# Three orders changed in an attention and routing tower: three TensorE matmuls, two ScalarE casts, one GpSimd chain

## The chip, the cores and the metric

One core of one Trainium2 chip. The metric is the device time of one execution in microseconds (us). Five engines work side by side and meet through semaphores: TensorE (PE; its weight loads have rows of their own, PEld), VectorE (DVE), ScalarE (ACT), GpSimd (POOL) and SyncE (SP, which only issues DMAs here).

## The reference, cut to what matters

`x` holds 128 samples of 375 x 512 floats. Each sample is cut into q, k and v of 125 rows each.

```python
weight = softmax(einsum('bct,bcs->bts', q * scale, k * scale))   # 512 x 512 for each sample
h = einsum('bts,bcs->bct', weight, v)                            # 125 x 512
h = h + attn(layernorm(h), Wq, Wk, Wv, Wo)                       # rotary, soft-capped tanh, 8 heads, 2 kv heads
y = layernorm(h)
out = h + (silu(y @ sw1) * (y @ sw3)) @ sw2                      # shared expert, width 448
        + top-2-of-8 experts of y                                # routed experts w1, w2, w3
```

All matmuls that matter keep 32-bit accuracy by splitting each operand into a high part (rounded to the fast 32-bit format of TensorE) and a low part (the rest), and multiplying high x high, high x low and low x high.

## The kernel before, in words

The kernel has two stages. The first, the tower, does one sample a step. The second runs the routed experts in groups of 512 rows. The change touches the tower alone.

A step `t` works on four samples at once, each at another point of its way: `has(0)` is sample t (512 x 512 scores, softmax, blend with v), `has(1)` is sample t-1, called a (first layernorm, qkv projection, rotary, attention), `has(2)` is sample t-2, called f (output projection, second layernorm, shared expert, routing), `has(3)` is sample t-3, called g (last part of the shared expert, output). There are 131 steps in all, 126 of which (t = 2 to 127) hold both a sample of `has(0)` and one of `has(2)`.

Each engine has its instructions for a step in an order written out by hand; nothing is planned at run time. An engine executes them in that order and stops at each `wait_ge` until the named semaphore has the value. So an instruction that is put earlier in the order of its engine can start earlier, and everything that it is moved past starts behind it.

The names that the change and its surroundings touch:

- TensorE: `scores(i)` (L433, three matmuls of 128 x 512) is one of four blocks of scores. `scores(2)` and `scores(3)` write into the PSUM bank from which ScalarE has to have read block 0 or 1 first (`e_sb`). `down_part(k, 1)` (L418) are matmuls of sample g's shared expert that write to bank 6. The transposes of X (L478), of `xn` and `y` (L408), the output projection `woT` (L345, 12 matmuls), the q part of `wqkv` (L345, 12 of width 512), the kv part (12 of width 256), and `turn_weights` (L444), which turns the normalised softmax weights `e`.
- ScalarE: `weights(i)` (L619) is the exponential of block i with its row sum; `vT_high` (L643) is the high part of the values, `xT_hi` (L599) the high part of the normed rows, which the q product waits for.
- VectorE: `h2` (L763, the profile prints it as `h<-ps,h`), its statistics `st` and `ag` (L770), `y` (L778, second layernorm), `rz` (L783) and the four `e<-e,rz` (L786), which scale the softmax weights and for which `turn_weights(0)` waits.
- GpSimd: `rstd(b, ...)` is two one-column operations, `ve` (variance plus epsilon, L904) and `rs` (its power -0.5, L907). It is called once for sample a (first layernorm) and once for sample f (second layernorm, for which `y` waits). `vT_low` (L931) is the low part of the values, 128 x 500, first read by TensorE in the blend near the end of the step. Then follow two indirect DMAs (L941) that write routing entries, `qkr` (L949) and `qk_low` (L916).

SyncE loads the next sample and stores two results of 250 KB in each step; none of its code is touched.

Of the kernel before, what the change touches and what calls it, by code (L numbers as in the profile page):

```python
# [25 lines left out]
ACT = mybir.ActivationFunctionType  # L26
# [45 lines left out]
def audio_tower(nc, x, wq, wk, wv, wo, gate_w, w1, w2, w3, sw1, sw2, sw3, expert_bias, cos, sin, out):  # L72
# [28 lines left out]
    with ExitStack() as ctx:  # L101
# [40 lines left out]
        vT = [sbuf(f"vT_{part}", [P, KC, C], F32R, tower) for part in ("high", "low")]  # L142
# [113 lines left out]
        def one(name, shape, dt=F32):  # L256
            return sbuf(name, shape, dt, tower)
# [9 lines left out]
        vT_full = one("vT_full", [P, KC, C])  # L267
# [3 lines left out]
        st2, ag2 = one("st2", [P, 6]), one("ag2", [P, 2])  # L271
        ve1, rs1 = one("ve1", [P, 1]), one("rs1", [P, 1])
        ve2, rs2 = one("ve2", [P, 1]), one("rs2", [P, 1])
# [36 lines left out]
        s_ps, o_ps, pv_ps = signal("s_ps", 2), signal("o_ps"), signal("pv_ps", 2)  # L310
        rank_ps, dn_ps, aT_ps = signal("rank_ps"), signal("dn_ps"), signal("aT_ps")

        xT_hi, vT_hi, yT_hi, v_sb, th_sb = (signal(n) for n in ("xT_hi", "vT_hi", "yT_hi", "v_sb", "th_sb"))
        ex_sb, e_sb, qkT_hi, hT_hi = signal("ex_sb"), signal("e_sb", KC), signal("qkT_hi"), signal("hT_hi")
        tanh_sb, p_sb = signal("tanh_sb", 2), signal("p_sb", 2)
        aT_hi, qk_hi, e_hi, vT_sb = signal("aT_hi"), signal("qk_hi"), signal("e_hi", KC), signal("vT_sb")

        h_sb, st1_sb, ag1_sb, xn_sb = signal("h_sb"), signal("st1_sb"), signal("ag1_sb"), signal("xn_sb")
        h2_sb, st2_sb, ag2_sb, y_sb = signal("h2_sb"), signal("st2_sb"), signal("ag2_sb"), signal("y_sb")
# [8 lines left out]
        ve1_sb, rs1_sb, ve2_sb, rs2_sb = signal("ve1_sb"), signal("rs1_sb"), signal("ve2_sb"), signal("rs2_sb")  # L328
# [37 lines left out]
        with nc.Block() as block:  # L366
# [37 lines left out]
            def _(pe):  # L404
# [7 lines left out]
                def step(t, has, n):  # L412
                    a, f, g = back(t, 1), back(t, 2), back(t, 3)
                    p = t[1] % 2

                    def down_part(k, part, c=0, last=False):

                        return nc.tensor.matmul(ps[0:C, 6, :], hT[c][0:HW, k, 0:C], w2s[part][0:HW, k, 0:D],  # L418
                                                start=(k == 0 and part == 0 and c == 0), stop=last)

                    def scores(i):

                        if i == 0:
                            pe.wait_ge(qk_hi.sem, qk_hi.at(t))
                            pe.wait_ge(qk_lo.sem, qk_lo.at(t))
                            pe.wait_ge(e_lo.sem, e_lo.at(a))
                        elif i == 1:
                            pe.wait_ge(h_sb.sem, h_sb.at(a))
                        else:
                            pe.wait_ge(e_sb.sem, e_sb.at(t, i - 1))  # L430
                        qk = (qk_high[p], qk_low)
                        for n_, (b, c) in enumerate(PASSES):
                            last = nc.tensor.matmul(ps[:, (i + 1) % 2, :], qk[b][0:C, 0, i * P:(i + 1) * P],  # L433
                                                    qk[c][0:C, 1, :], start=(n_ == 0), stop=(n_ == 2))
                        last.then_inc(qk_ps.sem, 1)
# [37 lines left out]
                    if has(0):  # L473
# [4 lines left out]
                            last = nc.tensor.transpose(ps[:, 2, k * C:(k + 1) * C],  # L478
                                                       X[p][0:C, 2, k * P:(k + 1) * P], ident[0:C, 0:C])
                        last.then_inc(vT_ps.sem, 1)  # L480
                    if has(0):
                        scores(2)
                    if has(3):
                        for k in range(1, HC):
                            down_part(k, 1)
                    if has(0):
                        scores(3)
                    if has(2):
# [108 lines left out]
            def _(act):  # L597
                def hi_part(dst, bank, rows):
                    return nc.scalar.activation(dst[0][0:rows, :, 0:C],  # L599
                                                ps[0:rows, bank, 0:KC * C].rearrange("p (k c) -> p k c", k=KC), ACT.Copy)  # L600
# [8 lines left out]
                def step(t, has, n):  # L609
                    a, f = back(t, 1), back(t, 2)  # L610
# [23 lines left out]
                    if has(0):  # L634
                        act.wait_ge(vT_ps.sem, vT_ps.at(t))
                        act.wait_ge(vT_lo.sem, vT_lo.at(a))
                        nc.scalar.activation(vT_full[:, :, :], ps[:, 2, 0:KC * C].rearrange("p (k c) -> p k c", k=KC),
                                             ACT.Copy).then_inc(vT_sb.sem, 1)
                        weights(2)
                        weights(3)  # L640
                        act.wait_ge(vT_sb.sem, vT_sb.at(t))
                        act.wait_ge(o_ps.sem, o_ps.at(a))
                        nc.scalar.activation(vT[0][:, :, :], vT_full[:, :, :], ACT.Copy).then_inc(vT_hi.sem, 1)  # L643
                    if has(1):
                        act.wait_ge(xT_ps.sem, xT_ps.at(a))
                        act.wait_ge(kv_ps.sem, kv_ps.at(f))
                        hi_part(xT, 3, P).then_inc(xT_hi.sem, 1)
                    if has(2):
                        act.wait_ge(yT_ps.sem, yT_ps.at(f))
                        act.wait_ge(up_ps.sem, up_ps.at(back(f, 1)))  # L650
                        hi_part(yT, 3, P).then_inc(yT_hi.sem, 1)
# [243 lines left out]
            @block.gpsimd  # L895
            def _(pool):
                last_entry = pool.to_reg(REGIONS - 1)

                def rstd(b, aggr, ve, rs, aggr_sb, ve_done, rs_done, rs_used):

                    pool.wait_ge(aggr_sb.sem, aggr_sb.at(b))
                    pool.wait_ge(rs_used.sem, rs_used.at(back(b, 1)))
                    alone(pool)
                    nc.gpsimd.tensor_scalar(ve[0:C, :], aggr[0:C, 1:2], EPS, None, ALU.add).then_inc(ve_done.sem, 1)  # L904
                    pool.wait_ge(ve_done.sem, ve_done.at(b))
                    alone(pool)
                    nc.gpsimd.tensor_tensor(out=rs[0:C, :], in0=ve[0:C, :], in1=mhalf[0:C, :],  # L907
                                            op=ALU.pow).then_inc(rs_done.sem, 1)

                def cut_scores(b):  # L910

                    q = b[1] % 2
                    pool.wait_ge(qk_hi.sem, qk_hi.at(b))
                    pool.wait_ge(qk_ps.sem, qk_ps.at(back(b, 1)))
                    alone(pool)
                    nc.gpsimd.tensor_tensor(out=qk_low[0:C, :, :], in0=X[q][0:C, 0:2, :],  # L916
                                            in1=qk_high[q][0:C, :, :].bitcast(F32),
                                            op=ALU.subtract).then_inc(qk_lo.sem, 1)

                def step(t, has, n):  # L920
                    a, f, g = back(t, 1), back(t, 2), back(t, 3)
                    if n == 0:
                        cut_scores(t)
                    if has(1):
                        rstd(a, ag1, ve1, rs1, ag1_sb, ve1_sb, rs1_sb, xn_sb)
                    if has(0):

                        pool.wait_ge(vT_hi.sem, vT_hi.at(t))
                        pool.wait_ge(o_ps.sem, o_ps.at(a))
                        alone(pool)  # L930
                        nc.gpsimd.tensor_tensor(out=vT[1][:, :, 0:C], in0=vT_full[:, :, :],  # L931
                                                in1=vT[0][:, :, 0:C].bitcast(F32),
                                                op=ALU.subtract).then_inc(vT_lo.sem, 1)
                    if has(2):
                        rstd(f, ag2, ve2, rs2, ag2_sb, ve2_sb, rs2_sb, y_sb)
                    if has(3):
                        pool.wait_ge(pick.sem, pick.at(g))
                        pool.wait_ge(place.sem, place.at(g))
                        alone(pool)
                        for k in range(2):  # L940
                            nc.gpsimd.indirect_dma_start(  # L941
                                routed, bass.IndirectOffsetOnAxis(ap=slot[g[1] % 2][0:C, k:k + 1], axis=0),
                                entry[k][g[1] % 2][0:C, :], None, bounds_check=last_entry,
                                oob_is_err=False).then_inc(scattered.of(g), 16)
                    if has(1):
                        pool.wait_ge(rope_sb.sem, rope_sb.at(a))
                        pool.wait_ge(rT_ps.sem, rT_ps.at(f))
                        alone(pool)
                        nc.gpsimd.tensor_tensor(out=qkr[0:C, :], in0=rc[0:C, :], in1=rsn[0:C, :],  # L949
                                                op=ALU.add).then_inc(rope_add.sem, 1)  # L950
                    if has(-1):
                        cut_scores(back(t, -1))
                each_step(pool, step)
                for b in ((0, NB - 2), (0, NB - 1)):
                    pool.wait_ge(scattered.of(b), scattered.at(b))
# [431 lines left out]
```

## Time and profile before

| | us |
|---|---|
| median of 3 runs | 6224.8 (6224.19 to 6226.47) |
| the profiled execution's own time | 6225.23 |
| its span in the trace | 6223.5 |
| TensorE busy | 6034.7 (97%) |
| VectorE busy | 3931.3 (63%) |
| ScalarE busy | 2617.3 (42%) |
| GpSimd busy | 2608.1 (42%) |

Busy time is the union of an engine's instructions. TensorE's matmuls are pipelined and their ends are modelled, so a wait of TensorE shows more fully before a weight load (PEld) than before a matmul. Times in the rows are counted from the span's start. The granted TensorE clock of the execution was 0.991 of full speed.

### The profile page before, as it was taken

What the parts mean: (1) busy time and instruction counts of PE and PEld (TensorE: products, weight loads), DVE (VectorE), ACT (ScalarE), POOL (GpSimd) and SP (SyncE); (2) the same over time, 40 slices, a digit from 0 to 9 for tenths busy, and PEclk for the clock granted to TensorE, in tenths of its full rate; (3) what the DMA queues carried; (4) which work ended last, traced back from release to release, by engine and by line L of the source; (5) the groups of instructions that cost most, each with busy time, mean ns of one, the idle gap of its engine ahead of it and who ended that gap; (6) DMA issues with size and microseconds to landing.
All of it is one profiled execution on the core that took longest, in us unless ns stands there. A gap on an engine that the chain in (4) does not pass through costs nothing. (4 is left out here: it accounts for less than half of the span.)

```text
span 6223.5 us, 108360 instructions
## 1 busy us (share of the span) xinstructions
PE 6034.7 (97%) x32968; PEld 5134.6 (83%) x32968; DVE 3931.3 (63%) x9812; ACT 2617.3 (42%) x4904; POOL 2608.1 (42%) x1865
## 2 busy tenths in 40 slices
PE   5999999999999999999999996999999999999999
PEld 4888888888888888888888885888888888888888
DVE  4777777777777777777777774444444444444444
ACT  3444444444444444444444442333333333333332
POOL 1333333333333333333333333555555655555554
PEclk8999999999999999999999998999999999999999
DMA  2111111111111111111111113555555555555541
GB/s 69 48 44 44 47 41 47 44 44 47 42 49 41 46 45 43 48 41 48 43 44 47 42 40 102 138 143 141 143 144 143 132 140 145 137 143 144 143 105 48
DMA packets 273407, 495.61 MB, mean 80 GB/s; under 512 B 39444, under 2 KB 112148, under 8 KB 273236
## 3 DMA queue, kind: packets, MB, share of 16 engines
q1 hardware_dynamic: 202452, 363.37, 19.6%
q0 software_dynamic: 70912, 131.71, 10.4%
q8 instruction: 22, 0.36, 0.0%
q14 instruction: 21, 0.17, 0.0%
HBM read 370.13 MB, written 140.28 MB: 82 GB/s over the span
## 5 line engine op out<-in xcount | busy, mean ns | idle before, releaser
L1325 POOL DMA_INDIRECT out_dram<-res,goal x280 | 519.4, 1855 | 929.9 <-DVE res L1261 446.1
L619 ACT ACTIVATE e<-ps,shift 128x512 f32<-128x512 f32 x512 | 347.9, 684 | 671.1 <-DVE shift L718 635.3
L1193 ACT ACTIVATE rT_hi<-ps 128x512 fp32r<-128x512 f32 x280 | 167.9, 600 | 1040.2 <-PE ps L1129 1040.2
L1119 PE MATMUL ps<-e_hi,rT_hi 128*128 128x448 f32 x2240 | 596.9, 388 | 5.2 <-ACT rT_hi L1193 5.2
L1303 POOL TENSOR_TENSOR e_lo<-raw,e_hi 128x1792 fp32r<-128x1792 f32 x140 | 568.6, 4062 | 9.8 <-ACT e_hi L1188 6.5
L1261 DVE COPY res<-ps 128x512 f32<-128x512 f32 x280 | 193.7, 692 | 594.8 <-PE ps L1119 579.8
L1119 PE MATMUL ps<-e_lo,rT_hi 128*128 128x448 f32 x2240 | 550.8, 367 | 0.0
L1119 PE MATMUL ps<-e_hi,rT_lo 128*128 128x448 f32 x2240 | 549.4, 367 | 0.0
L904 POOL TENSOR_SCALAR ve<-ag 125x1 f32<-125x1 f32 x256 | 57.1, 223 | 1124.7 <-DVE ag L734 1087.0
L1119 PEld LDWEIGHTS ps<-e_hi,rT_lo 128*128 128x128 f32 x2240 | 421.2, 188 | 37.8
L1119 PEld LDWEIGHTS ps<-e_lo,rT_hi 128*128 128x128 f32 x2240 | 421.2, 188 | 37.3
L931 POOL TENSOR_TENSOR vT_low<-vT_full,vT_high 128x500 fp32r<-128x500 f32 x128 | 164.8, 1287 | 588.4 <-ACT vT_high L643 588.4
L1275 DVE SCALAR_TENSOR_TENSOR ega<-eth,ps 128x448 f32<-128x448 f32 x280 | 174.0, 622 | 375.2 <-ACT eth L1214 369.1
L949 POOL TENSOR_TENSOR qkr<-rc,rsn 125x640 f32<-125x640 f32 x128 | 201.2, 1572 | 483.4 <-DVE rsn L814 483.4
L1119 PEld LDWEIGHTS ps<-e_hi,rT_hi 128*128 128x128 f32 x2240 | 380.5, 190 | 25.6 <-issue 5.6
L1214 ACT ACTIVATE eth<-ps,half 128x448 f32<-128x448 f32 x280 | 178.0, 636 | 516.7 <-PE ps L1119 515.0
L941 POOL DMA_INDIRECT routed_entries<-entry,slot x256 | 345.6, 1350 | 113.7 <-issue 100.9
L916 POOL TENSOR_TENSOR qk_low<-X,qk_high 125x1024 fp32r<-125x1024 f32 x128 | 307.2, 2400 | 203.7 <-ACT qk_high L606 203.7
L1188 ACT ACTIVATE e_hi<-raw 128x1792 fp32r<-128x1792 f32 (+1 forms) x210 | 372.6, 1774 | 40.3 <-DMA raw<-in_L_ffn_w 40.3
L715 DVE TENSOR_REDUCE negmax<-ps 128x1 f32<-128x512 f32 x512 | 341.1, 687 | 35.5 <-PE ps L433 22.0
L1282 DVE SCALAR_TENSOR_TENSOR egb<-ega,half,ps 128x448 f32<-128x448 f32 x280 | 190.5, 680 | 272.3 <-PE ps L1119 256.2
L626 ACT ACTIVATE e_cut_hi<-ps 128x512 fp32r<-128x512 f32 x512 | 277.2, 594 | 178.8 <-PE ps L444 177.6
(203 smaller groups left out, 15377.0 us busy)
## 6 DMA issues: line engine op xcount, KB each, us to landing
raw<-in_L_ffn_w SPq DMA_DIRECT2D x210, 896.0 KB, 5.6
X<-in_x SPq DMA_DIRECT2D x128, 750.0 KB
normed_rows<-y SPq DMA_DIRECT2D x128, 250.0 KB
out_dram<-h SPq DMA_DIRECT2D x128, 250.0 KB
rows<-normed_rows,entries POOLq DMA_INDIRECT x280, 4.8
out_dram<-res,goal POOLq DMA_INDIRECT x280
routed_entries<-entry,slot POOLq DMA_INDIRECT x256
raw<-in_L_ffn_sw SPq DMA_DIRECT2D x3, 896.0 KB
```

What stands on the lines that cost most here:

```text
L619: nc.scalar.activation(e[:, i, :], ps[:, (i + 1) % 2, :], ACT.Exp, scale=QS, bias=shift[:, i:i + 1], accum_out=total[:, i:i + 1]).then_inc ...
L626: nc.scalar.activation(e_cut[0][:, j, :], ps[:, j % 2, :], ACT.Copy).then_inc(e_hi.sem, 1)
L715: nc.vector.tensor_reduce(negmax[:, i:i + 1], ps[:, (i + 1) % 2, :], AX.X, ALU.max, negate=True).then_inc(max_sb.sem, 1)
L916: nc.gpsimd.tensor_tensor(out=qk_low[0:C, :, :], in0=X[q][0:C, 0:2, :], in1=qk_high[q][0:C, :, :].bitcast(F32), op=ALU.subtract).then_inc( ...
L941: nc.gpsimd.indirect_dma_start(routed, bass.IndirectOffsetOnAxis(ap=slot[g[1] % 2][0:C, k:k + 1], axis=0), entry[k][g[1] % 2][0:C, :], Non ...
L949: nc.gpsimd.tensor_tensor(out=qkr[0:C, :], in0=rc[0:C, :], in1=rsn[0:C, :], op=ALU.add).then_inc(rope_add.sem, 1)
L1119: ins = nc.tensor.matmul(dst, lhs[a][:rows_, k, :], rhs[b][:rows_, k, 0:width], start=(k == 0 and i == 0), stop=(k == KC - 1 and i == 2))
L1188: nc.scalar.activation(W[group[1] % 2][n][0][:], raws[n][:], ACT.Copy).then_inc(w_hi[n].sem, 1)
L1261: nc.vector.tensor_copy(res[i % 2][:], ps[:, 7, :]).then_inc(res_sb.sem, 1)
L1282: nc.vector.scalar_tensor_tensor(gb[i % 2][:], ga[:], half2[group[1] % 2][:, i:i + 1], ps[:, b + 1, 0:HID], ALU.mult, ALU.mult).then_inc(g ...
L1303: nc.gpsimd.tensor_tensor(out=W[group[1] % 2][n][1][:], in0=raws[n][:], in1=W[group[1] % 2][n][0][:].bitcast(F32), op=ALU.subtract).then_i ...
L1325: nc.gpsimd.indirect_dma_start(out, bass.IndirectOffsetOnAxis(ap=goal[group[1] % 2][:, i:i + 1], axis=0), res[i % 2][:], None, bounds_chec ...
```

## The change

Three blocks are moved to another place in the order of their engine. No instruction is added or removed.

```diff
 TensorE
-                    if has(0):
-                        scores(2)
                     if has(3):
                         for k in range(1, HC):
                             down_part(k, 1)
+                    if has(0):
+                        scores(2)
                     if has(0):
                         scores(3)
 ScalarE
                         weights(2)
                         weights(3)
+                    if has(1):
+                        act.wait_ge(xT_ps.sem, xT_ps.at(a))
+                        act.wait_ge(kv_ps.sem, kv_ps.at(f))
+                        hi_part(xT, 3, P).then_inc(xT_hi.sem, 1)
+                    if has(0):
                         act.wait_ge(vT_sb.sem, vT_sb.at(t))
                         act.wait_ge(o_ps.sem, o_ps.at(a))
                         nc.scalar.activation(vT[0][:, :, :], vT_full[:, :, :], ACT.Copy).then_inc(vT_hi.sem, 1)
-                    if has(1):
-                        act.wait_ge(xT_ps.sem, xT_ps.at(a))
-                        act.wait_ge(kv_ps.sem, kv_ps.at(f))
-                        hi_part(xT, 3, P).then_inc(xT_hi.sem, 1)
 GpSimd
                     if has(1):
                         rstd(a, ag1, ve1, rs1, ag1_sb, ve1_sb, rs1_sb, xn_sb)
+                    if has(2):
+                        rstd(f, ag2, ve2, rs2, ag2_sb, ve2_sb, rs2_sb, y_sb)
                     if has(0):
                         pool.wait_ge(vT_hi.sem, vT_hi.at(t))
                         pool.wait_ge(o_ps.sem, o_ps.at(a))
                         ...                       # vT_low, L931
-                    if has(2):
-                        rstd(f, ag2, ve2, rs2, ag2_sb, ve2_sb, rs2_sb, y_sb)
```

## Rows read from the trace of the kernel before

**Rows 1.** The page, busy time and share of the span of each engine.
```profile
PE 6034.7 (97%) x32968; PEld 5134.6 (83%) x32968; DVE 3931.3 (63%) x9812; ACT 2617.3 (42%) x4904; POOL 2608.1 (42%) x1865
```

**Rows 2.** One line's instructions, L643: durations in ns (min/median/max), first and last start.
```profile
L643 ACT ACTIVATE vT_high<-vT_full x128: 613/618/619, 68.7 to 3714.1; 128x500 fp32r<-128x500 f32 x128
```

**Rows 3.** Waits from 200 to 3700 us: us in total, times, longest.
```profile
PEld ps L433 <- ACT e L619: 86.9, 122, 0.8
...
PEld ps L345 <- issue: 31.9, 120, 0.3
```

**Rows 4.** Timeline of one step, weight loads: start, us, instruction [idle before <-releaser].
```profile
2011.64 0.58 PEld L478 LDWEIGHTS ps<-ident,X 125*128 125x128 f32 x4
...
2012.94 0.19 PEld L433 LDWEIGHTS ps<-qk_high 125*128 125x128 f32 x1 [0.72 <-ACT e L619]
...
2013.53 0.66 PEld L418 LDWEIGHTS ps<-w2s_lo,hT_hi 112*125 112x125 f32 x3
...
2014.22 0.19 PEld L433 LDWEIGHTS ps<-qk_high 125*128 125x128 f32 x1
...
2017.71 0.59 PEld L408 LDWEIGHTS ps<-ident,xn 125*128 125x128 f32 x4
...
2018.26 0.76 PEld L418 LDWEIGHTS ps<-w2s_hi,hT_lo 112*125 112x125 f32 x4
...
2019.29 0.75 PEld L345 LDWEIGHTS ps<-wqkv_hi,xT_hi 128*125 128x125 f32 x4 [0.27 <-issue]
...
2021.98 0.58 PEld L408 LDWEIGHTS ps<-ident,y 125*128 125x128 f32 x4
...
2024.15 0.86 PEld L444 LDWEIGHTS ps<-ident,e 128*128 128x128 f32 x8
```

**Rows 5.** Timeline of the same step, ScalarE.
```profile
2013.36 0.20 ACT L619 ACTIVATION_READ_ACCUMULATOR e<-ps,shift 128x1 f32 x1
...
2017.99 0.62 ACT L643 ACTIVATE vT_high<-vT_full 128x500 fp32r<-128x500 f32 x1
...
2018.57 0.59 ACT L599 ACTIVATE xT_hi<-ps 128x500 fp32r<-128x500 f32 x1
```

**Rows 6.** Timeline of the same step, VectorE and GpSimd.
```profile
2018.21 0.69 DVE L763 TENSOR_TENSOR h<-ps,h 125x512 f32<-125x512 f32 x1 [0.68 <-PE ps L345]
...
2018.81 1.29 POOL L931 TENSOR_TENSOR vT_low<-vT_full,vT_high 128x500 fp32r<-128x500 f32 x1 [4.51 <-ACT vT_high L643]
...
2019.82 0.18 DVE L770 BATCH_NORM_AGGREGATE ag<-st 125x2 f32<-125x6 f32 x1 [0.19 <-DVE st L766]
...
2020.27 0.22 POOL L904 TENSOR_SCALAR ve<-ag 125x1 f32<-125x1 f32 x1 [0.17 <-issue]
...
2020.68 0.57 POOL L907 TENSOR_TENSOR rs<-ve,mhalf 125x1 f32<-125x1 f32 x1 [0.18 <-POOL ve L904]
...
2021.38 0.55 DVE L778 TENSOR_SCALAR y<-h,ag,rs 125x512 f32<-125x512 f32 x1 [0.81 <-POOL rs L907]
2021.74 1.34 POOL L941 DMA_INDIRECT routed_entries<-entry,slot  x1 [0.50 <-issue]
...
2022.05 2.05 DVE L786 TENSOR_SCALAR e<-e,rz 128x512 f32<-128x512 f32 x4
```

**Rows 7.** Timeline of a window inside that group of four: its second instruction alone.
```profile
2022.45 0.86 DVE L786 TENSOR_SCALAR e<-e,rz 128x512 f32<-128x512 f32 x1
```

**Rows 8.** Timeline of step 0, where vT_low runs beside the scaling of e.
```profile
69.50 1.51 POOL L931 TENSOR_TENSOR vT_low<-vT_full,vT_high 128x500 fp32r<-128x500 f32 x1 [9.69 <-ACT vT_high L643]
69.83 1.46 DVE L786 TENSOR_SCALAR e<-e,rz 128x512 f32<-128x512 f32 x1
```

**Rows 9.** One line's instructions, L786, durations as in Rows 2.
```profile
L786 DVE TENSOR_SCALAR e<-e,rz x512: 467/482/1461, 69.0 to 3719.6; 128x512 f32<-128x512 f32 x171
```

**Rows 10.** Timeline of step 2, VectorE and GpSimd.
```profile
121.87 1.27 POOL L931 TENSOR_TENSOR vT_low<-vT_full,vT_high 128x500 fp32r<-128x500 f32 x1 [4.70 <-ACT vT_high L643]
123.11 0.22 POOL L904 TENSOR_SCALAR ve<-ag 125x1 f32<-125x1 f32 x1
...
124.79 1.68 DVE L786 TENSOR_SCALAR e<-e,rz 128x512 f32<-128x512 f32 x4
```

More of the change, by code:

```diff
@@ L640, in step @@
                         weights(3)
-                        act.wait_ge(vT_sb.sem, vT_sb.at(t))
-                        act.wait_ge(o_ps.sem, o_ps.at(a))
-                        nc.scalar.activation(vT[0][:, :, :], vT_full[:, :, :], ACT.Copy).then_inc(vT_hi.sem, 1)
                     if has(1):
@@ L647, in step @@
                         hi_part(xT, 3, P).then_inc(xT_hi.sem, 1)
+                    if has(0):
+                        act.wait_ge(vT_sb.sem, vT_sb.at(t))
+                        act.wait_ge(o_ps.sem, o_ps.at(a))
+                        nc.scalar.activation(vT[0][:, :, :], vT_full[:, :, :], ACT.Copy).then_inc(vT_hi.sem, 1)
                     if has(2):
```

## The prediction

> **What bounds the kernel now.** I read the page first. TensorE is busy for 97% of the span [rows 1], and the change only touches the tower, so the question is where TensorE stands still in one step of it. One instruction that each step holds once gives the period: the first start of `vT_high` is at 68.7 us, the last at 3714.1, with 127 steps between them, so 28.70 us a step [rows 2]. Next the waits: TensorE's weight loads wait for the exponential of block 0 in each of 122 steps, 86.9 us or 0.71 each, and in 120 steps 0.27 us ahead of a product of L345, put down to "issue" [rows 3]. Then the timeline of one step, which shows whether these waits are worth anything (times below are those of the step that begins near 2009; I leave the 2000 out). The first is ahead of `scores(2)`: the last transpose of X is loaded at 11.64 + 0.58 = 12.22, the scores start at 12.94. The second is ahead of the q product: the matmuls before it are loaded by 18.26 + 0.76 = 19.02, the product starts at 19.29 [rows 4]. `xT_hi` ends at 18.57 + 0.59 = 19.16 on ScalarE [rows 5], 0.13 before it. So I read the "issue" as the end of a wait for `xT_hi`: the pair of waits ahead of the product costs 0.13 after the cast. The reader is to see what follows: between the first stall and the second TensorE runs ahead of nothing. If the first stall goes alone, the second grows by the same amount.
>
> The third limit is not visible as a stall. `y` ends at 21.38 + 0.55 = 21.93 [rows 6], and TensorE loads it at 21.98, when its queue is also free (the product before takes 2.69). The scaling of `e` ends at 22.05 + 2.05 = 24.10 [rows 6], `turn_weights(0)` starts at 24.15 [rows 4]. Both are met to within 0.05 us. So in this step GpSimd's root, `y` and the four scalings form a chain that has no slack.
>
> **Part by part.**
>
> *Three matmuls ahead of `scores(2)`.* Their weight loads take 13.53 to 14.22, 0.69 [rows 4]; they fill the 0.72 of stall. `scores(2)` then starts at about 13.0 in place of 12.94, `scores(3)` at about 13.7 in place of 14.22 + 0.23; it needs exponential 1, which ends at 13.36 + 0.20 = 13.56 [rows 5]. Everything behind is up to 0.7 earlier, as far as the q product: the transposes of `xn` start at 17.0 in place of 17.71 and TensorE is free at 18.3 in place of 19.02. The output projection in between needs a cast that ScalarE starts behind exponential 1; with `xT_hi`'s 0.59 it is done by about 14.1, before the projection begins. By itself this part is worth 0, bounds 0 and 0.1 a step.
>
> *`xT_hi` ahead of `vT_high`.* ScalarE comes free at 17.99 and runs `vT_high` for 0.62 less overlap [rows 5]. With the order turned, `xT_hi` starts at 17.99, since the transposes of `xn` are now done by about 17.8, and ends at 18.58: 0.58 earlier. The q product starts at 18.71 in place of 19.29. With the first part this is -0.58 a step, bounds -0.4 (transposes late) and -0.7. `vT_high` ends at 19.2 in place of 18.61; behind it on ScalarE is only the cast of `y`.
>
> *The root of the second variance ahead of `vT_low`.* VectorE idles 0.68 ahead of `h2` [rows 6], so it can take nearly the whole advance: `h2` at 17.6, `ag` 0.6 earlier, `ve` at 19.67, `rs` from 20.08 to 20.65. Without this move `vT_low` would sit in front, so this keeps the chain early. What it costs is where `vT_low` lands. Before, it ran from 18.81 to 20.10, beside the statistics and `xT_lo` [rows 6]. Now its inputs are there long before and it starts when `rs` ends. GpSimd goes from one such operation to the next without a gap: `vT_low` from 121.87 for 1.27, the next at 123.11 [rows 10]. So `vT_low` holds 20.65 to 21.9. VectorE needs 0.13 from the end of `rs` to start `y` (20.68 + 0.57 = 21.25, `y` at 21.38), so `y` comes at 20.78, behind it.
>
> Step 0 shows what then happens. `vT_low` ran there beside the four scalings of `e`. The one that met it took 1.46 against a median of 0.48 [rows 8, 9], and ended at 71.29, 0.28 after `vT_low` did at 71.01. It was held for the whole rest of `vT_low`. The scalings are also held by the indirect DMAs of GpSimd: the second of four takes 0.86 [rows 7], and the group 2.05 against the 1.68 of a step without such DMAs [rows 6, 10]. `y` itself was never beside a GpSimd operation over the data. It belongs to the same form, I think: 512 elements from SBUF in 0.55, against 0.69 for `h2`, which reads PSUM [rows 6]. So `y` ends at 21.9 + 0.28 = 22.2 in place of 21.93. TensorE is ready for it at 21.4 and gets it at 22.2 + 0.13 = 22.32, in place of 21.98: +0.34. The 0.58 is given back, and a third of a us more.
>
> The Trainium skill, "SBUF — State Buffer", section "Who interferes with whom", says that VectorE in a two-port mode, which a `tensor_scalar` can enter, and a GpSimd operation shut each other out entirely, and that the one that issues first keeps the shared ports to its end. By that rule `y` waits as computed; if `y` were not of that form, the rule would leave it alone and only the scalings would meet `vT_low`. Rows 8 show the exclusion for `e`, none shows it for `y`.
>
> *Behind `y`.* The scalings start at about 22.3 and end at 22.3 + 2.05 = 24.35, since the DMAs now start at about 22.4 and still meet them; TensorE is ready for the transposes of `e` at 24.15 + 0.34 = 24.49. Hidden by 0.1; if the DMAs hold two scalings (0.38 each), it is 0.2 late. The DMAs' own shift of 0.7 is free: nothing on GpSimd follows until `qkr`, near 28.5, and `vT_low` is first read later than that. All that follows in the step hangs on TensorE and moves with it, so the +0.34 is the change of the period.
>
> **Sum.** 126 steps hold all parts: 126 x 0.34 = 43 us. On the profiled execution (6225.2, 0.4 above the median of the runs) that gives 6268; I take **6267**. The bounds of the terms give +0.2 to +0.5 a step: 6250 to 6288.
>
> **The rivals.**
>
> *No lockout, the gain stays.* If `y` and `vT_low` run side by side, or `vT_low` starts only after the scalings, the period falls by the 0.58 of the q product: 6225 - 126 x 0.58 = 6152. For it: `y` never showed a delay (nor had it occasion), and TensorE's stalls do lie where the three moves put them. Against: step 0. It decides at `y`: if it ends before 21.9, this comes in. 12%.
>
> *`y` first, the scalings held.* If GpSimd needs over 0.13 us to go from `rs` to `vT_low`, `y` runs from 20.78 to 21.33 and `vT_low` runs behind it to about 22.5. The first scaling ends at 22.8, the others at 23.9 to 24.4, where 24.10 was. TensorE was ready at 23.57. So -0.2 to +0.3 a step: 6200 to 6263, about 6232. For it: the DMA came 0.50 after `rs` [rows 6]. Against: the gapless pair of rows 10. 18%.
>
> *Worse.* `y` is held, and the scalings again, by the later DMAs: +0.55 a step, 6295. 5%.
>
> *The change doesn't do what it says.* If the transposes of `xn` are not done when ScalarE is free, or the advance of TensorE shrinks, the q product gains less than 0.58. That leaves `y` late just the same, since it hangs on `h2` and the root; the time stays in the forecast's range. 3%, to 6280.
>
> **How the numbers follow.** The forecast has 62%. The range of 6203 to 6288 leaves out the first rival and the worst one, and a part of the tails. Faster by over 0.2% (under 6212): the first rival's 12% and some of the second's low end, with a margin for what I overlooked in a chain this tight, 18%. Within 0.2%, about what can be told from no change: 12%, from the second rival. Slower: 70%.
>
> **What would show it.** In the profile after: the wait of L433 for `e` gone; `xT_hi` directly behind exponential 3, the q product 0.5 to 0.6 earlier from the step's start; a wait of 0.9 us ahead of the transposes of `y`; `y` at about 1.4 us in place of 0.55, in all steps from 2 on; `vT_low` directly behind `rs`; the four scalings still near 2.05. Wrong if `y` stays at 0.55: then the scalings tell which rival it is, at 2 us the first, at 3 us the second. Wrong in another way if TensorE's advance of 0.58 is not there at the q product.

## The result, and the profile after

The changed kernel takes 6253.6 us (median of 6 runs, 6247.4 to 6258.7), the kernel before 6225.7 beside it. The ratio is 1.0043, with a 95% interval of 1.0031 to 1.0055: slower by 28 us, 0.22 us in each of the 126 steps that hold all three parts. 6267 was forecast, in a range of 6203 to 6288. The profiled execution was the slowest of the six (6258.7, span 6256.9), so its trace shows 33 us and not 28.

First the same kind of row as [rows 2], of the changed kernel: the line of `vT_high` and, with it, those of `y` and of the scalings of `e`.

```profile
L648 ACT ACTIVATE vT_high<-vT_full x128: 614/624/624, 69.0 to 3748.5; 128x500 fp32r<-128x500 f32 x128
...
L779 DVE TENSOR_SCALAR y<-h,ag,rs x128: 546/1495/1505, 123.0 to 3800.6; 125x512 f32<-125x512 f32 x128
...
L787 DVE TENSOR_SCALAR e<-e,rz x512: 467/481/1461, 69.4 to 3753.7; 128x512 f32<-128x512 f32 x171
```

The steps take (3748.5 - 69.0) / 127 = 28.97 us against 28.70. That is the whole difference of the two spans. `y` takes 1.50 us in the median, where it took 0.55 [rows 6]; the scalings of `e` are as short as they were [rows 9]. `y` is long in all 126 steps that hold `vT_low` too, and has two lengths there: 1.40 to 1.42 in 60 of them and 1.50 in 66. It starts 0.14 after `rs` ends in the first and 0.03 in the second kind, and its end comes 0.28 to 0.29 after the end of `vT_low` in each of them.

The waits of TensorE's weight loads, 200 to 3700 us, columns as in [rows 3]:

```profile
PEld ps L408 <- DVE y L779: 97.9, 121, 0.9
...
PEld ps L345 <- issue: 45.2, 120, 0.4
...
PEld ps L444 <- DVE e L787: 42.7, 120, 0.4
...
PEld ps L433 <- ACT e L619: 26.5, 121, 0.3
```

The old stall ahead of the third block of scores has shrunk from 0.71 to 0.22 a step. Two new ones stand further down: 0.81 a step for `y`, 0.36 for the scalings. Now the timeline of one step of the changed kernel, which answers to the one in [rows 4 to 6]. Its scores begin at 2026.85; those of the step in [rows 4 to 6] began at 2009.48.

```profile
2026.85 0.19 PEld L433 LDWEIGHTS ps<-qk_high 125*128 125x128 f32 x1
...
2029.57 0.53 PEld L418 LDWEIGHTS ps<-w2s_lo,hT_hi 112*125 112x125 f32 x3
...
2030.31 0.19 PEld L433 LDWEIGHTS ps<-qk_high 125*128 125x128 f32 x1 [0.21 <-ACT e L619]
...
2034.93 0.69 DVE L764 TENSOR_TENSOR h<-ps,h 125x512 f32<-125x512 f32 x1
...
2035.35 0.59 ACT L599 ACTIVATE xT_hi<-ps 128x500 fp32r<-128x500 f32 x1
...
2036.07 0.75 PEld L345 LDWEIGHTS ps<-wqkv_hi,xT_hi 128*125 128x125 f32 x4 [0.37 <-issue]
...
2037.39 0.56 POOL L908 TENSOR_TENSOR rs<-ve,mhalf 125x1 f32<-125x1 f32 x1 [0.18 <-POOL ve L905]
...
2037.93 1.27 POOL L934 TENSOR_TENSOR vT_low<-vT_full,vT_high 128x500 fp32r<-128x500 f32 x1
...
2038.09 1.40 DVE L779 TENSOR_SCALAR y<-h,ag,rs 125x512 f32<-125x512 f32 x1 [0.80 <-POOL rs L908]
...
2039.55 0.41 PEld L408 LDWEIGHTS ps<-ident,y 125*128 125x128 f32 x4 [0.86 <-DVE y L779]
...
2039.61 2.10 DVE L787 TENSOR_SCALAR e<-e,rz 128x512 f32<-128x512 f32 x4
...
2040.88 0.55 PEld L345 LDWEIGHTS ps<-wqkv_hi,xT_lo 128*125 128x125 f32 x4
...
2041.77 0.31 PEld L444 LDWEIGHTS ps<-ident,e 128*128 128x128 f32 x3 [0.35 <-DVE e L787]
```

Counted from the first scores of its step, the changed kernel against the one before (us, one step of each):

| | before | after | |
|---|---|---|---|
| h2 starts | 8.73 | 8.08 | -0.65 |
| q product starts | 9.81 | 9.22 | -0.59 |
| rs starts | 11.20 | 10.54 | -0.66 |
| y starts | 11.90 | 11.24 | -0.66 |
| y ends | 12.45 | 12.64 | +0.19 |
| TensorE loads y | 12.50 | 12.70 | +0.20 |
| scalings end | 14.62 | 14.86 | +0.24 |
| TensorE loads e | 14.67 | 14.92 | +0.25 |

In both kernels `y` starts up to 0.2 earlier in other steps. The means of 110 steps say the same as the table: TensorE loads `e` at 14.59 before and at 14.87 after, +0.28.

So all three moves did what they were written for, down to the start of `y`. Then `y` took back 0.85. This is the lockout of the prediction: one engine's instruction cannot get on while the other engine's runs. `vT_low` starts at 2037.93, 0.02 before `rs` ends; `y` comes 0.14 after that end and is shown busy until 2039.49, 0.29 after `vT_low` ends at 2039.20. The reader should note how it looks: the held instruction has no idle time ahead of it, it is simply long. VectorE's busy time rose by 121 us (4052.4 against 3931.3) with the same instructions; 114 of them are `y`'s (184.2 against 70.0 in all), 6 the scalings'.

### The profile page after: what moved, and what is told of

It is laid out like the page before. It is cut to its first block and busy times, and to the rows that moved or that the text cites. A ratio compares the mean times of both kernels' runs of the same rounds, so it can differ in the third digit from the quotient of the medians.

```text
span 6256.9 us, 108360 instructions
## 1 busy us (share of the span) xinstructions
PE 6067.7 (97%) x32968; PEld 5105.1 (82%) x32968; DVE 4052.4 (65%) x9812; ACT 2605.7 (42%) x4904; POOL 2596.2 (41%) x1865
## 5 line engine op out<-in xcount | busy, mean ns | idle before, releaser
L725 DVE TENSOR_TENSOR e_cut_lo<-ps,e_cut_hi 128x512 fp32r<-128x512 f32 x512 | 329.2, 684 | 32.0 <-ACT e_cut_hi L626 32.0
```

The lines of the kernel that those rows point to most:

```text
L725: nc.vector.tensor_tensor(e_cut[1][:, j, :], ps[:, j % 2, :], e_cut[0][:, j, :].bitcast(F32), ALU.subtract).then_inc(e_lo.sem, 1)
```

## Experiments

Each was timed beside the kernel before. Its median was 6223.9 beside `vT_low` behind the DMAs, `vT_low` twice, TensorE's part alone and TensorE's and ScalarE's parts together, and 6226.2 beside the other four.

**The low part of the values behind the DMAs.** The changed kernel, GpSimd's order being root, DMAs, `vT_low`:

```diff
                     if has(2):
                         rstd(f, ...)
-                    ...                # vT_low
                     if has(3):
                         ...            # the two indirect DMAs
+                    if has(0):
+                        ...            # vT_low, with its waits
```

> The changed kernel with one thing moved: GpSimd's low part of the values goes behind the two indirect DMAs, so that it is no longer beside y and the scalings of e. Theory (y is locked out while vT_low runs): y falls back to 0.55 us, the 0.58 a step of the earlier q product is kept, about 6152 us, and at least 6170. Rival (the loss comes from the new order on TensorE or ScalarE, or from the root coming earlier): nothing changes against the changed kernel, about 6254.

Measured: 6146.1 us, ratio 0.9875 (0.9858 to 0.9891), within 6 us of the theory's number. In this kernel's timeline `y` and `vT_low` no longer meet:

```profile
2007.90 0.56 POOL L908 TENSOR_TENSOR rs<-ve,mhalf 125x1 f32<-125x1 f32 x1 [0.18 <-POOL ve L905]
...
2008.49 0.55 DVE L779 TENSOR_SCALAR y<-h,ag,rs 125x512 f32<-125x512 f32 x1 [0.65 <-POOL rs L908]
...
2011.94 1.28 POOL L943 TENSOR_TENSOR vT_low<-vT_full,vT_high 128x500 fp32r<-128x500 f32 x1
```

`vT_low` at 2011.94 runs beside VectorE instructions that read PSUM (`yT_lo`, 0.66 us there and 0.67 before); TensorE's waits for `y` and `e` are gone from the list, but for one wait for `y` in a single step. The kernel also holds its own counter-test. Step 2 has no DMAs yet, so `vT_low` stands directly behind `rs` in it, and there alone `y` is long:

```profile
124.64 0.56 POOL L908 TENSOR_TENSOR rs<-ve,mhalf 125x1 f32<-125x1 f32 x1 [0.18 <-POOL ve L905]
...
125.16 1.28 POOL L943 TENSOR_TENSOR vT_low<-vT_full,vT_high 128x500 fp32r<-128x500 f32 x1
125.23 1.50 DVE L779 TENSOR_SCALAR y<-h,ag,rs 125x512 f32<-125x512 f32 x1 [0.65 <-POOL rs L908]
```

The same three moves are worth -78 us with `vT_low` there, +28 with it one block earlier.

**vT_low twice.**

```diff
+        spare = one("spare", [P, KC, C])
...
                         alone(pool)
+                        nc.gpsimd.tensor_tensor(out=spare[:, :, 0:C], ...)    # same inputs
                         nc.gpsimd.tensor_tensor(out=vT[1][:, :, 0:C], ...)
```

> The changed kernel with vT_low computed a second time, into a spare tile, directly ahead of the real one: GpSimd works 1.27 us longer at this place, in a stretch where it otherwise idles 3.7 us later in the step. Theory: y is held for both, about 2.77 us in place of 1.50, and every step is 1.27 longer: 6254 + 126 x 1.27 = 6414 us. If the lock could be taken between the two, y is held by the first alone and the scalings by the second: 6350 to 6414. Rival (vT_low is hidden, its length does not matter): 6254.

Measured: 6342.4 us, 1.0191 (1.0174 to 1.0208), 89 us over the changed kernel in place of 160: 0.70 a step. It is the case named second, and it came out below the range given for it, 6350 to 6414. Timeline of this kernel:

```profile
2023.65 1.26 POOL L935 TENSOR_TENSOR spare<-vT_full,vT_high 128x500 f32<-128x500 f32 x1
...
2023.81 1.39 DVE L780 TENSOR_SCALAR y<-h,ag,rs 125x512 f32<-125x512 f32 x1 [0.80 <-POOL rs L909]
...
2024.87 1.45 POOL L938 TENSOR_TENSOR vT_low<-vT_full,vT_high 128x500 fp32r<-128x500 f32 x1
...
2025.32 2.72 DVE L788 TENSOR_SCALAR e<-e,rz 128x512 f32<-128x512 f32 x4
```

`y` slips in between the two, and now the second one is the longer, 1.45 in place of 1.27: it waited for `y`. Then it holds a scaling: the group takes 2.72 in place of 2.10. The 0.62 of that group is nearly all of the 0.70. Windows inside the group show its first and its fourth scaling alone, and the first DMA:

```profile
2025.32 1.29 DVE L788 TENSOR_SCALAR e<-e,rz 128x512 f32<-128x512 f32 x1
...
2026.53 1.28 POOL L946 DMA_INDIRECT routed_entries<-entry,slot  x1 [0.21 <-issue]
2027.32 0.72 DVE L788 TENSOR_SCALAR e<-e,rz 128x512 f32<-128x512 f32 x1
```

The first is held by `vT_low` for 0.81, the fourth by the DMA for 0.25, the other two take 0.47 each: 1.68 for the free group [rows 10] and 1.06 make 2.74. In the changed kernel only the second was held, by the DMA, for 0.44. So the second `vT_low` costs what it still covers of a scaling (0.81), and the later DMA holds a scaling for less. That is how 1.27 us more of GpSimd work became 0.62.

**y first.** The changed kernel with `vT_low` waiting for `y`:

```diff
                     if has(0):
+                        if has(2):
+                            pool.wait_ge(y_sb.sem, y_sb.at(f))
                         pool.wait_ge(vT_hi.sem, vT_hi.at(t))
```

> The changed kernel with one wait more: vT_low starts only when y is done, so that it meets the scalings of e in place of y. Theory (either is held, what counts is which of them TensorE needs first): y 0.55 us, one scaling about 1.5, the group of four about 2.8, TensorE waits ahead of the transposes of e and not of y; about 0.1 a step over the kernel before, 6237 us (6224 to 6270). If holding y was the whole loss and the scalings had slack: 6150.

Measured: 6219.9 us, 0.9991 (0.9982 to 1.0001), no change from before that these runs could tell, and 34 us under the changed kernel. The place is as expected, the time is 17 us under the 6237 and lies below the range given with it (6224 to 6270). Timeline:

```profile
2019.10 0.55 DVE L779 TENSOR_SCALAR y<-h,ag,rs 125x512 f32<-125x512 f32 x1 [0.81 <-POOL rs L908]
...
2019.77 2.70 DVE L787 TENSOR_SCALAR e<-e,rz 128x512 f32<-128x512 f32 x4
...
2019.93 1.47 POOL L936 TENSOR_TENSOR vT_low<-vT_full,vT_high 128x500 fp32r<-128x500 f32 x1 [0.96 <-DVE y L779]
...
2022.52 0.85 PEld L444 LDWEIGHTS ps<-ident,e 128*128 128x128 f32 x8 [0.74 <-DVE e L787]
```

`y` is short, the group of four pays with 2.70 (2.8 was expected), and TensorE waits ahead of `e` and not of `y`: 0.64 in the mean of 122 steps, 0.74 in the one shown. In the means of 110 steps it loads `e` at 14.56 after the scores, against 14.59 before, so nothing is won or lost. This was the second rival of the prediction, made to happen: its price there was 6232.

**The parts alone.** Each is the kernel before with one part (or two) of the diff above and nothing else.

TensorE's part alone:

```diff
-                    if has(0):
-                        scores(2)
                     if has(3):
                         for k in range(1, HC):
                             down_part(k, 1)
+                    if has(0):
+                        scores(2)
```

> The kernel before with only the three matmuls put ahead of the third block of scores. Theory (the stall there is covered by the wait for xT_hi behind it): the wait ahead of the q product grows from 0.27 to about 0.9 and the time stays at 6226, within 6. Rival (the stall of 0.7 is on the path): about 6226 - 126 x 0.5 = 6163.

Measured: 6205.7 us, 0.9969 (0.9957 to 0.9980), -18 us or 0.14 a step. The theory, no change within 6 us, was wrong by this much. Most of the stall did move as it said:

```profile
2009.42 0.58 ACT L599 ACTIVATE xT_hi<-ps 128x500 fp32r<-128x500 f32 x1
...
2010.13 0.76 PEld L345 LDWEIGHTS ps<-wqkv_hi,xT_hi 128*125 128x125 f32 x4 [0.90 <-issue]
...
2012.06 0.55 DVE L778 TENSOR_SCALAR y<-h,ag,rs 125x512 f32<-125x512 f32 x1 [1.22 <-POOL rs L907]
...
2012.72 2.04 DVE L786 TENSOR_SCALAR e<-e,rz 128x512 f32<-128x512 f32 x4
...
2014.28 0.55 PEld L345 LDWEIGHTS ps<-wqkv_hi,xT_lo 128*125 128x125 f32 x4
...
2014.82 0.86 PEld L444 LDWEIGHTS ps<-ident,e 128*128 128x128 f32 x8
```

The wait ahead of the q product is 0.89 a step, where it was 0.27. But this step's scores began at 2000.41: the q product comes 9.72 after them (9.81 before), and the transposes of `e` come 14.41 after them (14.67; in the means of 110 steps 14.40 and 14.59). The first of these is because `xT_hi` starts 0.51 after `vT_high` here and 0.57 before (medians), where it seems to have waited a little for the transposes of `xn` too. The second is the same 0.09 and, beyond it, that `h2`, and with it `y` and the scalings, came earlier by themselves (`h2` 8.07 in place of 8.73 after the scores, `y` 11.65 in place of 11.90), and the scalings had been the later of the two that `turn_weights` needs. Here TensorE goes from the kv product (loaded by 2014.83) to `e` without a gap; in the step of before there had been 0.13, too short to be listed as idle. Such a gap, 0.07 in the mean, stands in 115 of the 126 steps of the kernel before, and in 1 here.

ScalarE's part alone:

```diff
-                    if has(0):   ... vT_high
+                    if has(1):   ... xT_hi
-                    if has(1):   ... xT_hi
+                    if has(0):   ... vT_high
```

> The kernel before with only the ScalarE part: xT_hi ahead of vT_high. The transposes of xn are not earlier, so xT_hi gains nothing; vT_high, vT_low, the second root and y follow one after the other 0.9 later, y itself at 0.55: 6224 + 126 x 0.93 = 6341 us. Rival (xT_hi waits only for ScalarE): 0.58 a step faster at the q product and the loss at the root smaller, about 6224 to 6280.

Measured: 6335.6 us, 1.0180 (1.0163 to 1.0197), as the theory had it. `y` takes 0.55 there; it is late, not held:

```profile
2017.67 1.28 POOL L932 TENSOR_TENSOR vT_low<-vT_full,vT_high 128x500 fp32r<-128x500 f32 x1 [5.56 <-ACT vT_high L648]
...
2018.92 0.22 POOL L905 TENSOR_SCALAR ve<-ag 125x1 f32<-125x1 f32 x1
...
2020.03 0.55 DVE L779 TENSOR_SCALAR y<-h,ag,rs 125x512 f32<-125x512 f32 x1 [1.66 <-POOL rs L908]
```

TensorE's and ScalarE's parts together:

```diff
 the TensorE and ScalarE hunks of the change; GpSimd as before (vT_low, then the second root)
```

> The changed kernel without its GpSimd part: TensorE and ScalarE orders new, vT_low ahead of the second root as before. vT_high ends 0.58 later, so vT_low, then the root, then y come later. Theory: root at 21.1 to 21.67 in place of 20.68 to 21.25, y 0.42 later but not held, 6226 + 126 x 0.42 = 6279 us. So the GpSimd move still pays within the change (6279 against 6254). Rival (the GpSimd move is what costs the 28 us): 6226 or faster, down to 6152.

Measured: 6262.8 us, 1.0063 (1.0046 to 1.0080). A row of its waits (200 to 3700 us) and two of its timeline:

```profile
PEld ps L408 <- DVE y L779: 104.2, 121, 0.9
...
2009.22 0.63 ACT L648 ACTIVATE vT_high<-vT_full 128x500 fp32r<-128x500 f32 x1
...
2012.31 0.55 DVE L779 TENSOR_SCALAR y<-h,ag,rs 125x512 f32<-125x512 f32 x1 [1.65 <-POOL rs L908]
```

The sign and the place are right (`y` 0.55 long, TensorE waits 0.86 a step for it), the size was 0.31 a step in place of 0.42. The scores of this step began at 2000.25, so `vT_high` ends 9.60 after them where it ended 9.13 after them before: 0.47 later, and not the 0.58 of the expectation, since it overlaps `xT_hi` by 0.12.

GpSimd's part alone:

```diff
+                    if has(2):   rstd(f, ...)
                     if has(0):   ... vT_low
-                    if has(2):   rstd(f, ...)
```

> The kernel before with only the GpSimd part: the root of the second variance ahead of vT_low. Nothing upstream is earlier, so the root comes when it came before, and vT_low meets y. Theory (lockout): y held to 1.5 us in every step, 0.9 later, nothing to pay for it with: 6224 + 126 x 0.9 = 6337 us. Rival (the root ahead is harmless or good by itself, the loss was in the combination): 6224 or less.

Measured: 6341.3 us, 1.0185 (1.0168 to 1.0202); the theory had 6337. `y` in this kernel:

```profile
2025.95 1.27 POOL L933 TENSOR_TENSOR vT_low<-vT_full,vT_high 128x500 fp32r<-128x500 f32 x1
...
2026.11 1.40 DVE L778 TENSOR_SCALAR y<-h,ag,rs 125x512 f32<-125x512 f32 x1 [0.80 <-POOL rs L907]
...
2027.57 0.41 PEld L408 LDWEIGHTS ps<-ident,y 125*128 125x128 f32 x4 [0.90 <-DVE y L778]
```

Alone, the lockout costs its full price, 115 us or 0.91 a step. The parts do not add up: -18, +109 and +115 by themselves, +28 together.

**One step further.** On top of the version with `vT_low` behind the DMAs, VectorE's maxima ahead of `xn`:

```diff
+                    if has(0):
+                        maxima(1)
                     if has(1):
                         ...            # xn
-                    if has(0):
-                        maxima(1)
```

> The version with the values' low part behind the DMAs, and on VectorE the maxima of blocks 2 and 3 ahead of xn. The exponentials 2 and 3 and with them xT_hi no longer wait for xn's 0.54. xn comes 1.4 later, at 16.65 in the time of the step of before, and TensorE asks for it at about 17.1, so xT_hi is then bound by the transposes of xn, 0.1 earlier than now: 6146 - 126 x 0.1 = 6133 us. Rival (xn is late for TensorE, or its transposes): 6146 or up to 6180.

Measured: 6140.4 us, 0.9864 (0.9847 to 0.9880). The direction fits. It was timed beside other runs of the kernel before than the 6146.1 (6140.9 to 6147.3), and the two intervals of the ratio overlap, so a gain of this edit is not shown. From its waits, 200 to 3700 us:

```profile
PEld ps L345 <- issue: 31.6, 120, 0.3
...
PEld ps L444 <- DVE e L787: 1.9, 12, 0.2
```

The wait ahead of the q product is down from 45.5 us in 120 steps, 0.12 a step, and waits for the scalings that are long enough to be listed come up in 12 steps. In the means of 110 steps the q product comes at 9.11 after the scores in place of 9.21, but the transposes of `e` at 13.92 in place of 13.93: the 0.1 that was expected is there at the q product and is lost again in front of `e`. The chain of `y` and the scalings sets the pace again. This is the fastest kernel run, 1.4% under the one before.

## Why the prediction was right, point by point

*What bounds the kernel.* Right in the large: TensorE stands still in one place because another holds it later. The reading of the 0.27 "issue" as a wait for `xT_hi` holds, since the wait grows to 0.90 when only TensorE's part is in. Wrong in two details. First, I took `y` and the scalings for equally tight; the scalings alone set the step. TensorE's way from `y` to `e` was shown as 2.17 us, and 0.13 of it was a wait for the scalings; and the 0.05 from the end of `y` to its load is the least of all steps, where the mean is 0.12. Second, the 0.13 from `xT_hi` to the q product was put down to its pair of waits; the load of `y` stands behind a pair of waits as well (`y` and `xT_lo`) and comes 0.05 after `y` where `y` is the later, so the reason is another, and open.

*Three matmuls ahead of the scores: 0 to 0.1 a step.* Measured alone 0.14. Missed were two small gains: the q product comes 0.09 earlier, and the transposes of `e` 0.26 in the step shown and 0.20 in the mean, since the scalings come earlier with `h2`. The stall did not vanish either, 0.22 of it is left: the three loads were counted with 0.69 and take 0.53 there (2029.57). `scores(3)` had begun at 14.22 [rows 4], not 0.23 later as the prediction has it; it now begins at 13.61 in that count, 13.7 was forecast.

*xT_hi first: the q product 0.58 earlier.* 0.59.

*The root first, and where vT_low lands.* Right in order and in mechanism: `vT_low` gets in ahead of `y`, `y` ends 0.29 after it (0.28 was taken from step 0), in the steps from the third on. The end of `y` was put at 12.72 after the scores, it was 12.64, since the root was 0.07 earlier than computed.

*The sum, +0.34 a step.* Measured +0.27 in the trace and +0.22 by the median times. Two terms were mis-sized, besides the 0.08 at the end of `y`. I gave TensorE 0.13 from the end of `y` to its load, the figure of the q product; it was 0.06. So `y` was loaded 0.20 later than before and not 0.34. And the scalings were called hidden by 0.1 behind a kv product that ends 2.17 after `y` is loaded; after the stall it took 1.88, so TensorE was there early and waited 0.35 for them. They ended at 14.86, where I had put 14.87. It is they that set the step: 14.92 against 14.67, +0.25. The two errors partly make up for each other, too much at `y` and nothing for the scalings, and that is luck. The mechanism, `y` longer by 0.85 to 0.95 at this place, is not.

*The rivals.* "No lockout" is refuted in this kernel and is what it becomes when `vT_low` is moved: 6146, for which 6152 was worked out. "`y` first" was not what happened; forced, it gave 6220, inside the 6200 to 6263 that were given for it. The margin by which GpSimd won was as read: no gap from `rs` to `vT_low`, 0.14 from `rs` to `y` in the step shown.

The rule of the Trainium skill, "SBUF — State Buffer", section "Who interferes with whom", that the one which issues first keeps the ports to its end, agrees with the traces in both directions: `y` held by `vT_low` (1.50 in place of 0.55), `vT_low` held by `y` (1.45 in place of 1.27). One number is left open: `y` needs 0.55 by itself and ends only 0.28 to 0.29 after the recorded end of `vT_low`. Whether it had done a part before, or `vT_low` lets go ahead of its recorded end, no run here shows. That `y` is in a two-port mode is not measured by itself either; what is shown is that it is held, and that the statistics (0.69 us, with or without it) and `xT_lo` (0.65, with or without it), which ran beside the `vT_low` of 2018.81 to 2020.10 in the kernel before [rows 6], were not:

```profile
2018.93 0.69 DVE L766 BATCH_NORM_STATS2 st<-h 125x6 f32<-125x512 f32 x1
...
2019.92 0.65 DVE L704 TENSOR_TENSOR xT_lo<-ps,xT_hi 128x500 fp32r<-128x500 f32 x1
```

## What to carry to other kernels

Before moving work on GpSimd, list which VectorE instructions it will run beside at its new place, and what TensorE waits for among them. An operation that is far off the critical path can be the dearest one in the step if it locks out a short one that is on it; put it beside VectorE work that was not held here, such as the instructions that read PSUM. Several small advances are worth testing one by one and together: here each of two parts alone cost over 100 us, and all three with one block moved further gained 78.

## What the runs showed of the hardware

- GpSimd's next tensor operation wins against VectorE's use of the result. `vT_low` started 0.02 to 0.03 us before the recorded end of `rs`, `y` 0.03 or 0.14 after it, in all 126 steps. It does not hold for whatever stands there: with an indirect DMA behind `rs`, the DMA started 0.48 after it (2008.94), and `y` was first (2008.49).
- The lockout shows as duration and not as idle time: 0.91 us a step in the mean, 114 us over 126 steps, stood in VectorE's busy time, and no wait of VectorE names it.
- The first indirect DMA, too, holds a scaling, for 0.38 us in [rows 7]. The held one ends 1.51 to 1.56 us after the start of the DMA in nearly all steps, and when the DMA moves, the hold moves with it: it is the second scaling in the changed kernel (0.92 us) and the fourth with `vT_low` twice (0.72); with `y` first the group is over before that moment and the DMA holds none.
- An indirect DMA follows `vT_low` by 0.22 us where it follows the small `rs` by 0.50 [rows 6].
